# Attention of the second layer in two halves of heads, key masking on GpSimd, and five smaller moves

## The chip, the cores and the metric

The kernel runs on one core of a Trainium2 chip. The metric is the device time of one execution in microseconds, the median of three runs. The core has TensorE (PE in the profile; PEld is its weight load), VectorE (DVE), ScalarE (ACT), GpSimd (POOL) and SyncE (SP), which issues most of the DMAs. Each engine works through its own program in order, and they wait for each other on semaphores.

## The reference

Two transformer layers over 64 blocks (batch entries) of 128 tokens with 256 features, 16 heads of 16 features. Both attend to a context of 128 rows per block. Layer 1 has a mixture of 64 experts behind its attention, layer 2 a gated feed-forward with values rounded to 8 bits.

```python
x = x + tanh(g_xattn[0]) * L0_xattn(layernorm(x), ctx, ctx)            # stage 1
x = x + tanh(g_ffn[0])   * L0_ffn(layernorm(x))                        # stage 2: experts + shared expert
x = x + tanh(g_xattn[1]) * L1_xattn(layernorm(x), ctx, ctx, mask)      # stage 3
x = x + tanh(g_ffn[1])   * L1_ffn(layernorm(x))                        # stages 4 and 5

def L1_xattn(q, k, v, mask):
    query, key, value = heads(q @ wq.T + bq), heads(k @ wk.T + bk), heads(v @ wv.T + bv)
    scores = where(mask == 0, -1e9, query @ key.T / sqrt(16))
    return softmax(scores) @ value @ wo.T + bo

def L1_ffn(x):
    xq = fake_quant(x, clip_x)                                         # needs the maximum of all of x
    h  = fake_quant(silu(xq @ w_gate.T) * (xq @ w_up.T), clip_down)    # needs the maximum of all of h
    return h @ w_down.T
```

## The kernel before

The program has five stages: attention of layer 1, experts, attention of layer 2, pass 0 (gate, up and product of the feed-forward, and its maximum) and pass 1 (rounding, down projection, output). `phase_end` (L269) drains an engine and waits for all five; it stands after the constants (1), after the attention of layer 1 (2), after that of layer 2 (4) and after pass 0 (5).

**Attention.** `attention_pe`, `attention_act`, `attention_dve` and `attention_sp` serve both layers (L is 0 or 1; the profile's stage 3 is L = 1). A block goes through *slots*: in slot s each engine runs its `body` once, each step on the block `stage(lag)` = s - lag. The letters are n (lag -2), g (-1), f (0), m (1), k (2), o (3), w (4), v (5), u (6). The order inside `body` is written out by hand.

A block's scores for all 16 heads take four PSUM banks, `tiles` [128, 4, 512]. Four heads' rows of 32 partitions (two heads of 16, the other masked to zero) lie in four row groups; `scores` (L429) issues for each row group i and half j a matmul of 32 rows and 256 columns into bank i. `maximum` (L933) reduces all four banks to 16 maxima per token with one DVE instruction. `maxima_t` transposes them, `shifted` (L944) adds them to the queries in `qm`. `scores_t` (L446) computes the scores again, transposed, with the maximum taken off, into the same four banks, 16 matmuls of 32 rows and 128 columns. `exponent` (L692) writes their exponential to `pt` with one ACT instruction. In layer 2 `masks` (L421) first writes the mask bias to the banks, before both. `values` (L475) multiplies by the values (16 matmuls into four column groups of 32), `heads_to_tokens` (L561), `head_sums` and `head_norm` (L1038, L1047) and `tokens_to_heads` (L571) normalise, `output` (L544) projects, `residual` (L957) adds. `transposes` (L491) and `project_qk` (L510) make the queries of the coming blocks.

In layer 2 the keys were computed before and come back by DMA (`load_keys_values`, L1216); ACT spreads them into `kp` with four instructions (`mask_keys`, L725), each key copy with the other head's features masked. GpSimd's loop (L2121) does the inverse root of the norm for slot s (`inverse_roots`), adds the experts' outputs of the next block (`experts_sum`, for which DVE's `first_sum` waits) and adds the bias (`add_bias`).

The order of TensorE's body in layer 2 is scores(m), values(o), project_qk(f), transposes(g), scores_t(k), heads_to_tokens(o), output(w), tokens_to_heads(o), maxima_t(m). Scores of m wait for the exponential of k's predecessor, scores_t(k) for the maximum of m: one set of banks serves both.

**The seams.** At the start SP issues the first tile of the context and of x, then eight weight DMAs (`w_in`, L1976), and ends phase 1. GpSimd waits for all of `w_in` (L2083) and clears rows in DRAM with three DMAs (L2104); DVE waits for `w_in` too and runs `scale_queries` (L1993) before the first norm. At the end of layer 2 all engines drain (`phase_end(…, 4)`); then ACT rounds the first chunk of pass 0 (L1794), and in the second chunk's slot calls Silu once on `silu_ready` (L1811), which loads its table. In pass 1 ACT rounds a chunk of 512 tokens in six parts, DVE converts them in three pairs (`whole`, L1907), and TensorE's `down` (L1935) starts when all three pairs are there.

## Time and profile before

| | us |
|---|---|
| median of three runs (lowest, highest) | 1837.52 (1836.88, 1838.45) |
| the profiled execution | 1842.04 |
| its span, first to last instruction | 1840.3 |
| busy in the span: TensorE, DVE, ACT, GpSimd | 1720.2, 1382.6, 1169.1, 668.5 |
| granted TensorE clock, mean | 0.983 |

Attention of layer 1 takes the time up to about 620 us, the experts up to about 1125, attention of layer 2 up to about 1630, pass 0 up to 1756 and pass 1 the rest. The rows further down come from one profiled execution. Times are microseconds from the start of its span; in rows grouped by line the last figure of the mean is nanoseconds. "L527" is line 527. Matmuls overlap, so a busy TensorE is not a full one: the distance from the start of one group to the start of the next says more. A float32 matmul is recorded as two instructions.

### The profile page before, as it was taken

What the parts mean: (1) busy time and instruction counts of PE and PEld (TensorE: products, weight loads), DVE (VectorE), ACT (ScalarE), POOL (GpSimd) and SP (SyncE); (2) the same over time, 40 slices, a digit from 0 to 9 for tenths busy, and PEclk for the clock granted to TensorE, in tenths of its full rate; (3) what the DMA queues carried; (4) which work ended last, traced back from release to release, by engine and by line L of the source; (5) the groups of instructions that cost most, each with busy time, mean ns of one, the idle gap of its engine ahead of it and who ended that gap; (6) DMA issues with size and microseconds to landing.
All of it is one profiled execution on the core that took longest, in us unless ns stands there. A gap on an engine that the chain in (4) does not pass through costs nothing.

```text
span 1840.3 us, 54611 instructions
## 1 busy us (share of the span) xinstructions
PE 1720.2 (93%) x20134; PEld 1343.9 (73%) x20144; DVE 1382.6 (75%) x4582; ACT 1169.1 (64%) x2411; POOL 668.5 (36%) x750
## 2 busy tenths in 40 slices
PE   5999999999999799999999998999999999968845
PEld 4888888888887688888888886677777777733334
DVE  4899999999998546655555544788888888759988
ACT  3777777777777233333323334788888888858875
POOL 1111111111111147777777774222222222211157
PEclk9999999999999899999999998999999999989989
DMA  3233333333334569888988885233332333203274
GB/s 104 83 95 95 95 98 107 98 96 101 98 95 153 173 187 233 220 223 206 223 216 217 216 178 154 83 96 93 89 88 88 89 94 95 69 35 138 103 279 178
DMA packets 231350, 247.64 MB, mean 135 GB/s; under 512 B 29680, under 2 KB 207216, under 8 KB 228912
## 3 DMA queue, kind: packets, MB, share of 16 engines
q1 hardware_dynamic: 206272, 205.54, 34.8%
q0 software_dynamic: 24816, 38.62, 11.6%
q8 instruction: 163, 2.67, 0.6%
q14 instruction: 99, 0.81, 0.1%
HBM read 142.40 MB, written 101.66 MB: 133 GB/s over the span
## 4 chain that ended last, share of the span: by engine, by line
PE 72%; DVE 17%; ACT 8%; issue 1%; SPq 1%; POOL 0%; DMA 0%; POOLq 0%; DVEq 0%; ACTq 0%
DVE mt L940 8%; PE tiles L459 8%; PE tiles L442 8%; PE bank L527 7%; ACT pt L699 6%; PE bank L403 6%; PE tiles L1464 6%; PE bank L383 6%; PE bank L487 4%; PE bank L557 3%; PE tiles L426 3%; PE bank L1478 3%; PE bank L540 3%; PE bank L413 3%; DVE hmax L1852 3%; PE tiles L1446 2%
## 5 line engine op out<-in xcount | busy, mean ns | idle before, releaser
L2091 POOL TENSOR_TENSOR rstd<-var,minus_half 128x2 f32<-128x2 f32 x140 | 97.9, 700 | 650.8 <-DVE var L1020 634.8
L940 DVE TENSOR_REDUCE mt<-tiles 128x16 f32<-128x2048 f32 x128 | 293.5, 2293 | 54.2 <-PE tiles L442 54.1
L699 ACT ACTIVATE pt<-tiles 128x2048 f32<-128x2048 f32 x128 | 240.7, 1880 | 48.1 <-PE tiles L459 48.1
L1639 POOL DMA_INDIRECT accumulator<-ye,tid x128 | 208.5, 1629 | 84.6 <-DVE ye L1583 54.3
L1583 DVE TENSOR_SCALAR ye<-bank,xr 128x256 f32<-128x256 f32 x128 | 56.1, 480 | 154.6 <-PE bank L1478 154.6
L2102 POOL TENSOR_TENSOR res<-res,bias 128x256 f32<-128x256 f32 x128 | 92.9, 725 | 205.8 <-ACT xn L758 203.1
L1624 POOL DMA_INDIRECT xr<-token_rows,tid x128 | 136.9, 1070 | 72.6 <-issue 35.1
L527 PE MATMUL bank<-xt,w_q 128*128 128x128 f32 x1024 | 155.2, 285 | 1.4 <-ACT xt L707 1.4
L459 PE MATMUL tiles<-qm,qkp 32*128 32x128 f32 x4096 | 151.1, 284 | 2.6 <-DVE mt L940 2.6
L442 PE MATMUL tiles<-qkp 32*128 32x256 f32 x2048 | 151.2, 409 | 1.8 <-ACT qkp L721 1.6
L459 PEld LDWEIGHTS tiles<-qm,qkp 32*128 32x128 f32 x4096 | 126.7, 187 | 28.4 <-issue 24.5
L527 PEld LDWEIGHTS bank<-xt,w_q 128*128 128x128 f32 x1024 | 131.9, 195 | 15.6 <-issue 13.6
L487 PE MATMUL bank<-pt,vx 128*32 128x128 f32 x4096 | 140.1, 278 | 1.6 <-ACT at L790 1.0
L487 PEld LDWEIGHTS bank<-pt,vx 128*32 128x32 f32 x4096 | 105.2, 110 | 44.5 <-issue 41.1
L557 PE MATMUL bank<-w_o,at 128*128 128x256 f32 x512 | 133.1, 383 | 1.7 <-ACT at L790 1.7
L952 DVE SCALAR_TENSOR_TENSOR qm<-bank,keep,qkp 128x256 f32<-128x256 f32 x256 | 111.1, 476 | 15.7 <-PE bank L473 15.6
L442 PEld LDWEIGHTS tiles<-qkp 32*128 32x128 f32 x2048 | 87.8, 186 | 40.8 <-issue 27.5
L719 ACT ACTIVATE qkp<-bank,qb 128x128 f32<-128x128 f32 x256 | 88.7, 372 | 36.3 <-PE bank L527 36.2
L675 ACT ACTIVATE res<-bank 128x256 f32<-128x256 f32 x64 | 24.5, 383 | 135.5 <-PE bank L403 135.5
L721 ACT ACTIVATE qkp<-bank,kb,keep 128x128 f32<-128x128 f32 x256 | 106.1, 483 | 0.0
L734 ACT ACTIVATE qkp<-cxax,kb,keep 128x128 f32<-128x128 f32 x256 | 105.4, 485 | 0.0
L557 PEld LDWEIGHTS bank<-w_o,at 128*128 128x128 f32 x512 | 88.0, 192 | 9.5 <-ACT at L790 2.9
(247 smaller groups left out, 4079.9 us busy)
## 6 DMA issues: line engine op xcount, KB each, us to landing
keys_values<-res SPq DMA_DIRECT2D x64, 256.0 KB, 2.9
cxax<-keys_values SPq DMA_DIRECT2D x128, 128.0 KB, 2.5
cxax<-accumulator SPq DMA_DIRECT2D x128, 128.0 KB, 2.2
hidden_away<-h_ring SPq DMA_DIRECT2D x8, 1536.0 KB, 5.0
token_rows<-pay SPq DMA_DIRECT2D x64, 160.0 KB, 1.8
pt<-in_expert_up SPq DMA_DIRECT2D x36, 256.0 KB, 3.5
cxax<-in_ctx SPq DMA_DIRECT2D x64, 128.0 KB, 2.2
res<-in_x SPq DMA_DIRECT2D x64, 128.0 KB, 2.3
```

Of the source, the lines that this page charges most:

```text
L383: last = nc.tensor.matmul(kv_bank(n)[:, k * D:(k + 1) * D], weights_, moving, start=(c == 0), stop=(c == KC - 1))
L403: last = nc.tensor.matmul(shared_bank(n)[:, m * FS + j * P:m * FS + (j + 1) * P], w[:, c, j * P:(j + 1) * P], sxt[n % SHARED_IN][:, c, :], ...
L442: last = nc.tensor.matmul(both, qt[r % 2][rows, j, :], kp[r][rows, :, j, :], start=(L == 0), stop=True, skip_group_check=(L == 1))
L459: last = nc.tensor.matmul(tiles[:, i, n * P:(n + 1) * P], kp[r][rows, e, j, :], qm[rows, e, j, :], start=(L == 0), stop=True, skip_group_c ...
L487: last = nc.tensor.matmul(bank[7][32 * h:32 * h + 32, g * P:(g + 1) * P], vx[r][:, GH * g + h, :], pt[p][:, i, n * P:(n + 1) * P], start=T ...
L527: last = nc.tensor.matmul(o_, w[:, c, j * P:(j + 1) * P], (cx[r] if n else xt[p])[:, c, :], start=(c == 0), stop=(c == KC - 1))
L557: last = nc.tensor.matmul(bank[6][:, 0:D], at[r % 2][:, c, :], w_o[:, c, :], start=(c == 0), stop=(c == KC - 1))
L699: nc.scalar.activation(pt[r % 2][:, :, :], tiles[:, :, :], ACT.Exp).then_inc(sem("exp_done"), 1)
L940: nc.vector.tensor_reduce(mt[:, :].rearrange("p (i n c) -> p i n c", i=RT, n=2 * KC)[:, :, :, 0], tiles[:, :, :].rearrange("p i (n k) -> p ...
L952: last = nc.vector.scalar_tensor_tensor(qm[:, e, :, :], bank[4][:, MAXC[L]:MAXC[L] + P].unsqueeze(1).broadcast_to([P, KC, P]), keep[:, 1 - ...
L1624: nc.gpsimd.indirect_dma_start(out=xr[n % ROWS_IN][:, h, :], out_offset=None, in_=rows[:, :], in_offset=bass.IndirectOffsetOnAxis(ap=tid[n ...
L1639: nc.gpsimd.indirect_dma_start(out=acc[p][:, :], out_offset=bass.IndirectOffsetOnAxis(ap=tid[b % 8][:, h:h + 1], axis=0), in_=ye[r][:, h, ...
```

## The change

**Layer 2.** The 16 heads are treated as two halves h, each in two of the four banks (`tiles[:, 2h:2h+2]`). `half_step(h, m, k, between)` writes both masks, then issues the scores of half h of one block together with the transposed scores of the other half of an older one. Each goes in two pieces u: two row groups serve the scores and the other two the transposed scores, then the roles change; in between stands the work `between`, then a wait of TensorE for the landing of its own first piece. Maximum, exponential and values are cut in two as well. `qm` gets a second buffer in the place of `w_k`. The residual moves one slot back. GpSimd masks the keys. `s_done` and `st_done` now count four per block, `max_done` and `exp_done` two.

```diff
+            def half_step(h, m, k, between):
+                if m is not None:
+                    b, r = m
+                    wait(pe, "exp_done", NB + 2 * (b - 2) + h + 1 if b >= 2 else 0)
+                    mask_half(h, 0)
+                    pe.wait_ge(sem("qk_out_1"), 2 * b + h + 1)
+                    pe.wait_ge(sem("keys_masked"), b + 1)
+                if k is not None:
+                    bt, rt = k
+                    ht_ = 1 - h
+                    pe.wait_ge(sem("max_done"), NB + min(2 * (bt + 1) + ht_ + 1, 2 * NB))
+                    mask_half(ht_, 1)
+                    pe.wait_ge(sem("qm_done"), NB + bt + 1)
+                for u in range(2):
+                    if u == 1:
+                        between()
+                        if m is not None:
+                            pe.wait_ge(sem("s_done"), NB + 4 * b + 2 * h + 1)
+                        if k is not None:
+                            pe.wait_ge(sem("st_done"), NB + 4 * bt + 2 * ht_ + 1)
+                    for e in range(2):
+                        for a_ in range(2):
+                            if m is not None:
+                                i = 2 * a_ + u
+                                rows = slice(32 * i, 32 * i + 32)
+                                n = 2 * u + e
+                                s_last = nc.tensor.matmul(tiles[:, 2 * h + a_, n * P:(n + 1) * P], qt[r % 2][rows, h, :], kp[r][rows, e, h, :],
+                                                          start=False, stop=True, skip_group_check=True)
+                        for a_ in range(2):
+                            if k is not None:
+                                i = 2 * a_ + 1 - u
...
+                    if m is not None:
+                        s_last.then_inc(sem("s_done"), 1)
+                    if k is not None:
+                        t_last.then_inc(sem("st_done"), 1)
...
                 else:
-                    values(o)
+                    half_step(0, m, o, lambda: tokens_to_heads(w))
                     project_qk(f)
                     transposes(g)
-                    scores_t(k)
+                    values_half(0, o)
+                    half_step(1, m, k, lambda: values_half(1, o))
+                    output(w)
                     heads_to_tokens(o)
-                    output(w)
-                    tokens_to_heads(o)
                     maxima_t(m)
...
                 else:
-                    mask_keys(f)
                     normalise_first(g)
                     normalise_second(u)
+                    copy_v(f)
+                    copy_at(w)
+                    exponent_half(1, o)
+                    copy_qk(f)
+                    copy_xt(g)
                     copy_ov(o)
-                    copy_qk(f)
-                    copy_v(f)
-                    copy_xt(g)
-                    exponent(k)
-                    copy_at(o)
+                    exponent_half(0, k)
...
                 else:
-                    maximum(m)
                     first_sum(n)
+                    maximum_half(0, m)
                     first_stats(n)
+                    residual(v)
+                    second_stats(v)
                     variances(n, y)
                     norming(1)
                     token_maximum(u)
+                    maximum_half(1, m)
+                    norming(1)
                     head_sums(o)
                     head_norm(o)
-                    residual(w)
-                    second_stats(w)
                     shifted(m)
-                    norming(1)
...
+            def mask_keys(b):
+                if not 0 <= b < NB:
+                    return
+                r, p = b % 4, b % 2
+                pool.wait_ge(sem(f"kv_in{p}"), 16 * (b - p) + 32)
+                pool.wait_ge(sem("st_done"), NB + 4 * max(b - 3, 0))
+                for j in range(KC):
+                    for e in range(2):
+                        last = G.tensor_scalar(kp[r][:, e, j, :], kvt[p][:, j * P:(j + 1) * P], keep[:, e:e + 1], kb[:, e, j:j + 1],
+                                               ALU.mult, ALU.add)
+                last.then_inc(sem("keys_masked"), 1)
+
             for s in range(NB + PAIR[1]):
                 inverse_roots(pool, 1, s)
+                mask_keys(s - 1)
                 experts_sum(s + 1)
                 add_bias(pool, 1, s)
```

**Norm.** At the start x is loaded before the context; GpSimd no longer waits for the weights, and DVE waits for them and scales the queries only after the first tile's statistics. **Clearing.** The three clearing DMAs of GpSimd move to slot 8 of layer 1. **Drain.** GpSimd no longer drains at the end of layer 2. **Table.** ACT calls Identity once before phase 1 ends and Silu once before phase 4 ends; the call in pass 0 goes. **First chunk.** In pass 1 the first chunk's down projection goes by pairs.

```diff
+                if L == 0 and stage(-2) is not None and stage(-2)[0] == 0:
+                    dve.wait_ge(sem("w_in"), 16 * 8)
+                    scale_queries(dve, 0)
...
-            for dump in (acc[0], acc[1], rows):
-                w = dump.shape[1]
-                G.dma_start(dump[T:T + HALVES * P, :].rearrange("(n p) d -> p n d", p=P), zt[:, :, 0:w]).then_inc(sem("dumps_zero"), 16)
             for s in range(FIRST[0], NB + LAGS):
                 add_bias(pool, 0, s - 2)
                 inverse_roots(pool, 0, s - FIRST[0])
+                if s == 8:
+                    for dump in (acc[0], acc[1], rows):
+                        w = dump.shape[1]
+                        G.dma_start(dump[T:T + HALVES * P, :].rearrange("(n p) d -> p n d", p=P), zt[:, :, 0:w]).then_inc(sem("dumps_zero"), 16)
...
-            phase_end(pool, 4)
+            pool.wait_ge(sem("rstd_step_1"), NORM_STEPS * (NB + PAIR[1] - 1) + 2)
+            pool.sem_inc(sem("phase_done"), 1)
+            pool.wait_ge(sem("phase_done"), PHASES[4])
...
+            act.wait_ge(sem("pool_made"), 3)
+            nc.scalar.activation(silu_ready[:, :], ident[:, 0:1], ACT.Identity)
             phase_end(act, 1)
...
             attention_act(act, 1)
+            act.wait_ge(sem("gates_out"), 1)
+            nc.scalar.activation(silu_ready[:, :], tg[:, 0:1], ACT.Silu)
             phase_end(act, 4)
...
+            def first_down():
+                for p in range(IC // 2):
+                    pe.wait_ge(sem("f_whole"), p + 1)
+                    for t in range(TPC):
+                        for i in (2 * p, 2 * p + 1):
+                            last = nc.tensor.matmul(bank[4 + t][:, 0:D], f_q[0][:, i, t * P:(t + 1) * P], wdi[:, i, :],
+                                                    start=(i == 0), stop=(i == IC - 1))
+                        if p == IC // 2 - 1:
+                            last.then_inc(sem("f_down_done"), 1)
```

## Rows read from the trace of the kernel before

**Rows 1.** Windows of 40 us: window, length, busy of each engine (instructions), clock, DMA, GB/s

```profile
1280.00:1320.00 40.00, 39.26 (x720) 28.73 (x717) 33.33 (x74) 34.49 (x72) 11.34 (x16) 1.00 0.30 88
```

**Rows 2.** Chain of waits by line, 1300 to 1320 us, layer 2

```profile
by line: DVE mt L940 34.6%; ACT pt L699 28.3%; PE tiles L442 16.8%; PE tiles L459 11.5%; PE tiles L426 11.0%; issue 1.7%
```

**Rows 3.** Timeline of TensorE, one slot of layer 2: start, us, engine, line, operation

```profile
1302.19 1.15 PE L442 MATMUL tiles<-qkp 32*128 32x256 f32 x16
1303.27 1.08 PE L487 MATMUL bank<-pt,vx 128*32 128x128 f32 x32
1304.28 1.16 PE L527 MATMUL bank<-xt,w_q 128*128 128x128 f32 x8
1305.27 0.38 PE L507 MATMUL bank<-ident,xn 128*128 128x128 f32 x2
1305.75 0.44 PE L426 MATMUL tiles<-mask_bias,identb 32*32 32x512 bf16 x16
1306.12 1.17 PE L459 MATMUL tiles<-qm,qkp 32*128 32x128 f32 x32
1307.22 0.66 PE L568 MATMUL bank<-ident,ovs 128*128 128x128 f32 x4
1307.72 1.03 PE L557 MATMUL bank<-w_o,at 128*128 128x256 f32 x4
1308.69 0.44 PE L578 MATMUL bank<-ident,on 128*128 128x128 f32 x2
...
1309.29 0.44 PE L426 MATMUL tiles<-mask_bias,identb 32*32 32x512 bf16 x16
1309.66 1.15 PE L442 MATMUL tiles<-qkp 32*128 32x256 f32 x16
```

**Rows 4.** Groups by line, 1200 to 1600 us: busy us, mean ns, idle before

```profile
L940 DVE TENSOR_REDUCE mt<-tiles 128x16 f32<-128x2048 f32 x54 | 123.8, 2293 | 16.0 <-PE tiles L442 16.0
L699 ACT ACTIVATE pt<-tiles 128x2048 f32<-128x2048 f32 x54 | 101.4, 1877 | 37.6 <-PE tiles L459 37.6
L734 ACT ACTIVATE qkp<-cxax,kb,keep 128x128 f32<-128x128 f32 x212 | 87.3, 485 | 0.0
```

**Rows 5.** Timeline of TensorE, three stages of a slot of layer 1

```profile
403.56 0.38 PE L588 MATMUL bank<-ident,pay 128*128 128x128 f32 x2
403.84 0.41 PE L507 MATMUL bank<-ident,xn 128*128 128x128 f32 x2
404.18 1.17 PE L459 MATMUL tiles<-qm,qkp 32*128 32x128 f32 x32
```

**Rows 6.** Groups of GpSimd by line, whole run

```profile
L2102 POOL TENSOR_TENSOR res<-res,bias 128x256 f32<-128x256 f32 x128 | 92.9, 725 | 205.8 <-ACT xn L758 203.1 <-DVE bias L2021 2.6
...
L1824 POOL CAST xq_b<-xq_f 128x1024 bf16<-128x1024 int8 x15 | 15.6, 1040 | 89.7 <-ACT xq_f L1794 89.7
```

**Rows 7.** Chain of waits in order of time, the first 20 us

```profile
5.27 3.55 DMA bias<-in_L_xattn_wo_b
...
11.96 0.75 POOL rstd L2091
13.05 1.28 ACT L758
...
17.00 3.78 PE bank L527 x16
```

**Rows 8.** Timeline at the end of layer 2 and the start of pass 0

```profile
1631.75 0.23 DVE L1667 TENSOR_SCALAR s_gux<-s_gu,scl 128x12 f32<-128x12 f32 x1
1633.29 2.19 ACT L1794 ACTIVATE xq_f<-big,scl 128x1024 int8<-128x1024 f32 x2 [3.85 <-POOLq L271]
...
1636.90 0.99 ACT L1802 COPY xqt<-bank 128x1024 bf16<-128x1024 bf16 x1
```

**Rows 9.** First chunk of pass 1: a row of the timeline, and one of the chain

```profile
1757.55 0.69 DVE L1914 CAST xq_f<-wgi 128x1024 bf16<-128x1024 int8 x1 [1.52 <-ACT wgi L1883]
...
1760.77 5.29 PE bank L1941 x24
```

More of the change, by code:

```diff
@@ L419, in attention_pe, with mask_half @@
             first = L * NB
-            def masks(n):
-                for i in range(RT):
+            def mask_half(h, n):
+                for i in (2 * h, 2 * h + 1):
                     rows = slice(32 * i, 32 * i + 32)
@@ L433, in scores @@
                 b, r = m
-                wait(pe, "exp_done", first + b - 1)
-                if L == 1:
-                    masks(0)
+                wait(pe, "exp_done", b - 1)
                 for j in range(KC):
@@ L441, in scores @@
                         both = tiles[:, i, :].rearrange("p (e c t) -> p e c t", e=2, c=KC)[:, :, j, :]
-                        last = nc.tensor.matmul(both, qt[r % 2][rows, j, :], kp[r][rows, :, j, :],
-                                                start=(L == 0), stop=True, skip_group_check=(L == 1))
+                        last = nc.tensor.matmul(both, qt[r % 2][rows, j, :], kp[r][rows, :, j, :], start=True, stop=True)
                 last.then_inc(sem("s_done"), 1)
@@ L450, in scores_t @@
                 b, r = k
-                pe.wait_ge(sem("max_done"), first + ahead(b, 2))
-                if L == 1:
-                    masks(1)
-                pe.wait_ge(sem("qm_done"), first + b + 1)
+                pe.wait_ge(sem("max_done"), ahead(b, 2))
+                pe.wait_ge(sem("qm_done"), b + 1)
                 for j in range(KC):
@@ L715, in copy_qk @@
                 act.wait_ge(sem("qk_done"), first + b + 1)
-                wait(act, "st_done", first + b - 3)
+                if L == 0:
+                    wait(act, "st_done", b - 3)
                 wait(act, "qm_done", first + b - 1)
@@ L723, in copy_qk @@
                     last.then_inc(sem(sm("qk_out")), 1)
-            def mask_keys(f):
-                if f is None:
-                    return
-                b, r = f
-                p = r % 2
-                act.wait_ge(sem(f"kv_in{p}"), 16 * (b - p) + 32)
-                wait(act, "st_done", first + b - 3)
-                for j in range(KC):
-                    for e in range(2):
-                        nc.scalar.activation(kp[r][:, e, j, :], kvt[p][:, j * P:(j + 1) * P], ACT.Identity, bias=kb[:, e, j:j + 1], scale=keep[:, e:e + 1])
             def copy_v(f):
@@ L1809, in body @@
                         quantise(stage(0))
-                        if stage(1) == 0:
-                            nc.scalar.activation(silu_ready[:, :], sig[:, 0:1], ACT.Silu)
                     if i == 4:
```

67 lines of the change are left out of this document (52 added, 15 removed).

## The prediction

> **What bounds the kernel now.** I read the stretches of the run first, then the chain of waits, then single slots. The program has five stages: attention of layer 1, experts, attention of layer 2, and two passes of the last feed-forward. The change works on the third, and on four seams: the start, the end of layer 2, the first chunk of pass 0 and that of pass 1.
>
> In layer 2 no engine is full: of 40 us TensorE shows 39.26, DVE 33.33, ACT 34.49 [rows 1]. The chain of waits says why [rows 2]: it goes round masks and scores, maximum, masks and transposed scores, exponential, all on the same four PSUM banks. Its round is from one scores start to the next, 1309.66 - 1302.19 = 7.47 us [rows 3]. The pieces fit: masks .37 and scores till they have landed 1.15, maximum 2.29, masks .37 and transposed scores 1.17, exponential 1.88 [rows 3, 4] make 7.23, and the rest are hand-overs. TensorE fills its free time in this chain with values, projection, transposes and output. "39.26 of 40" must not be read as full: ends are modelled. The reader should look at starts.
>
> **How much TensorE work there is in a slot.** From start to start [rows 3]: scores 1.08, values 1.01, projection .99, transposes of the next tile .48, masks .37, transposed scores 1.10, heads to tokens .50, output .97, then .60 for three transposes up to the masks, then .37. In layer 1, where nothing waits, two transposes take .28, and .34 where the next stage has another tiling [rows 5]. So of the .48 some .14 is waiting for the maximum, of the .97 some .05 for the normalised heads, of the .60 some .17 for the exponential: about .36 in all. The work is 7.47 - .36 = 7.11 us.
>
> **The change in layer 2.** With halves the maximum of one half runs beside the exponential of the other, and both beside TensorE. The chain no longer closes: after the second part of the first half step come projection, transposes and half the values (.99 + .34 + .56 = 1.89 us), against half an exponential (.94 and some .1 fixed) and half a maximum (1.15 and .1). After the second half step come output and heads to tokens, 1.38 us, against the same 1.25 and a landing of .1. That is just enough. So the .36 of waiting goes, and what is late next is TensorE's own work.
>
> That work grows. Scores (8 matmuls of 256 columns) and transposed scores (16 of 128) become four pieces of 8 matmuls of 128 columns, with other work between the pieces; values are cut in two. The transposed scores are 16 matmuls in 1.10 [rows 3]. Four matmuls run side by side, one in each row group; each is written as two records of 284 ns. First start to last end is 1.17, so the eighth group of records starts 1.17 - .284 = .89 after the first, about .115 per group with .08 more for the first (it waits for its weights), and the next stage starts .21 after that, .1 more than a group's time. A piece of half the size is then .08 + 4 x .115 + .10 = .64, not .55. Values have no such first step: 1.01 whole, 1.01 - 4 x .115 = .55 half. Piece by piece, in the new order: masks .37, piece .64, tokens to heads .33, piece .64, projection .99, transposes .34, half values .55, masks .37, piece .64, half values .55, piece .64, output .95, heads to tokens .43, one transpose .20: 7.64 us. Before it was 7.11, so .53 is added, for four more changes of tiling: half step | tokens to heads | half step, half step | half values | half step, and the two ends. I take these full, since TensorE works in order and rows 3 and 5 show the steps at every such boundary, whether it had waited or not.
>
> The new wait of TensorE on its own first piece (s_done, st_done) has the inserted work as cover: the piece lands .07 after the inserted one starts, which lasts .33 or .55. It costs nothing; without the inserted work it would cost about .3 twice a slot. Behind it stand all later matmuls.
>
> A rule speaks against this change: the Trainium skill, TensorEngine Tiling (Array Packing), Tiling Modes, says that changing the tiling mode drains the engine. By that rule the four boundaries are paid, as in my 7.64. Another page, the Trainium skill, TensorE: Matmul & The Clock Gate, Part 3, prices concurrent tiles at one matmul's duration and about 4 ns per tile more, and by that alone halves cost half, and the slot would be the 7.11 of the first rival.
>
> ACT loses four key masks (4 x .485 = 1.9) and gains one fixed part: 34.49 / 40 x 7.47 = 6.4 falls to about 4.7. DVE gains one fixed part of about .1: 33.33 / 40 x 7.47 = 6.2 becomes 6.4 [rows 1, 4]. It has slack against 7.64, but little where order matters: maximum, small norm, head sums, head norm, shift, first sum must pass in the 3.5 us from half step to half step. Keys masked, GpSimd: no row shows such an instruction. Bounds are 1024 one-input elements in 1.04, which is .13 for 128, and .73 for a whole two-input instruction of 256 [rows 6]; half of the latter, .36, is nearest, so 4 x .36 = 1.5 us per slot. Behind the four stands the sum of the experts' outputs (.73), for which DVE's first sum waits, and behind that one the maximum. Between the variance and the first sum of the next slot DVE's order has token maximum, half maximum, small norm, head sums, head norm and shift, over half of a slot of 7.64, about 4.0 us with its wait; .70 (inverse root) + 1.5 + .73 = 2.9 fits. It fits up to .64 per instruction; above that each .1 costs .4 a slot. SP's loads now wait for masks made two slots earlier: nothing.
>
> Slots: 64, of which three run while the pipeline fills and the clock is lower. 61 x (7.64 - 7.47) = +10.4. Filling brings longer TensorE slots at 1.2 GHz, and GpSimd's four instructions ahead of norm steps: -1 to +3, I take +1; draining has half exponentials but the same number of slots: 0.
>
> **The seams.** *Start.* The first inverse root came at 11.96, behind the weights, which land at 5.27 + 3.55, and behind three clearing DMAs of GpSimd, since GpSimd and DVE waited for the weights [rows 7]. Now the norm needs only x, whose load is issued first. The phase ends at about 5.9, after SP's last issue at 5.27, so the first inverse root is at about 7 and the first tile is normalised at 8.6; the 1.28 of table load is past by then. Then the value projection is last (weights 8.9, slow clock, to 11.0), its copy, transposes, copy of xt: projection at about 12.6 and not 17.00. -4.4, bounds -3 and -5. Clearing at slot 8 goes into GpSimd, which is idle most of a layer-1 slot: 0; with no such idle time 2.5.
>
> *Drain and table.* Pass 0 starts rounding at 1633.29, released by GpSimd's drain, though DVE's scales are ready at 1631.98 [rows 8]. Without it DVE's own drain is next, about 1632.1: -1.2. The Silu table no longer delays the copy at 1636.90, which could start at about 1636.4: -.5. Loaded earlier it lies under DVE's last steps.
>
> *First chunk of pass 1.* TensorE began at 1760.77, after the third pair, and ran 5.29 us to 1766.06 at the slow level, while the first pair was ready at 1758.24 [rows 9]. By pairs it does a third (1.76) at 1758.3, and ends about 1763.6. DVE's next steps take back a little: -2.0, bounds 0 (if ACT's rounding is what holds chunk two) and -2.4. Seams together -8.1, bounds -5 and -9.
>
> **Sum.** +10.4 + 1 - 8.1 = +3.3. Against the profiled execution, 1842.0 becomes 1845.3; its span is 1840.3, and the median of the runs is 4.5 lower than the profiled one, so the median goes from 1837.5 to about 1841.
>
> **The rivals.**
> *Half pieces cost half (0.30).* If drains and first weight loads overlap with neighbouring stages, TensorE's work stays near 7.11, at most 7.35. For it: between transposes and transposed scores in layer 1 only .06 is seen [rows 5]. Against it: the .21 between a row-tiled piece's last start and the next stage, in both layers. Time: 61 x (-.36 to -.12) + 1 - 8.1 gives 1808 to 1823, centre 1816.
> *The engines catch on each other (0.17).* The other side: DVE's stretch of 3.5 us has almost no slack, and the single transpose waits for the second half maximum. If each slot loses a further .2 at the hand-over DVE to TensorE before that transpose, the slot is 7.85, and +23 + 1 - 8.1 gives 1853. It decides from the point where half a maximum takes over 1.3 us, or the first sum ends later than the first half's scores.
> *GpSimd is late (0.06).* At .8 per mask instruction, .6 a slot are lost: over 1875.
> *It doesn't do what it says (0.02).* If the halves still ran one after another, two fixed parts more, 7.8: 1850.
> My forecast, TensorE-bound at 7.64, has 0.45. Its own range is 7.53 to 7.76: 1834 to 1849.
>
> **How the numbers follow.** 0.2% is 3.7 us, about what a measurement of this kernel can tell from no change: 1833.8 to 1841.2. The forecast's case gives same 0.20, slower 0.22, faster 0.03. The first rival gives faster 0.30, the second slower 0.15 and same 0.02, the others slower 0.08. Together faster 0.33, same 0.22, slower 0.45. The range is 1814 to 1857: it leaves out the lower part of the first rival and most of the late GpSimd.
>
> **What would show it.** Right: a layer-2 slot of 7.6 to 7.7; TensorE's stages start to start without idle time before the masks; each half piece .62 to .66; DVE waiting for scores before each half maximum; first projection near 12.6; pass 0 rounding about 1.2 us after DVE's last scale minus .1. Wrong: half pieces of .55 and a slot near 7.1 (first rival), idle time of TensorE before the single transpose or the masks released by DVE (second), DVE's first sum waiting for GpSimd (third). Most at risk is the .09 that each half piece is over half of a whole: 1 us in the sum is .016 per slot.

## The result, and the profile after

| | before | after | ratio, 95% interval |
|---|---|---|---|
| median of the runs (4 each) | 1837.99 us | 1864.38 us | 1.0145 [1.0126, 1.0163] |
| range of the runs | 1836.88 to 1838.91 | 1862.45 to 1872.07 | |
| profiled execution | 1842.04 | 1862.74 | |
| its span | 1840.3 | 1861.0 | |

The changed kernel is slower by 1.45%: 26.4 us between the medians, 20.7 between the two profiled executions. What follows explains the 20.7, which can be laid out stretch by stretch. The other 5.7 is the spread of single executions around their medians, and no trace shows it.

**A slot of layer 2.** First the window of 40 us, as in [rows 1], and the shares of the chain of waits, as in [rows 2]. Columns of the window: length, then busy us of TensorE, its weight loads, DVE, ACT and GpSimd with their instructions, the granted clock, the share of DMA, GB/s.

```profile
1280.00:1320.00 40.00, 40.00 (x781) 29.59 (x777) 32.16 (x78) 27.01 (x53) 19.25 (x35) 1.00 0.31 90
```

```profile
by line: PE tiles L457 31.7%; PE bank L581 16.3%; PE bank L540 14.4%; PE tiles L427 10.9%; PE bank L611 10.6%; PE bank L632 5.5%; PE bank L622 4.4%; PE bank L561 3.3%; PE tiles L464 2.7%; PE bank L511 1.5%
```

DVE and ACT, which held 34.6% and 28.3% of the chain before [rows 2], are gone from it. It is TensorE alone, from stage to stage. The next rows are one slot on TensorE, as [rows 3] were before: start, us, engine, line. L427 are the masks, L457 and L464 a piece of scores and of transposed scores side by side, L632 tokens to heads, L581 projection, L561 transposes, L540 half the values, L611 output, L622 heads to tokens, L511 the transpose of the maxima.

```profile
1299.93 0.43 PE L427 MATMUL tiles<-mask_bias,identb 32*32 32x512 bf16 x16
1300.29 0.38 PE L457 MATMUL tiles<-qkp 32*128 32x128 f32 x2
...
1300.50 0.28 PE L457 MATMUL tiles<-qkp 32*128 32x128 f32 x2
...
1300.62 0.28 PE L457 MATMUL tiles<-qkp 32*128 32x128 f32 x2
...
1300.95 0.44 PE L632 MATMUL bank<-ident,on 128*128 128x128 f32 x2
1301.31 0.38 PE L457 MATMUL tiles<-qkp 32*128 32x128 f32 x2
...
1301.97 1.16 PE L581 MATMUL bank<-xt,w_q 128*128 128x128 f32 x8
1302.97 0.38 PE L561 MATMUL bank<-ident,xn 128*128 128x128 f32 x2
1303.28 0.65 PE L540 MATMUL bank<-pt,vx 128*32 128x128 f32 x16
1303.85 0.43 PE L427 MATMUL tiles<-mask_bias,identb 32*32 32x512 bf16 x16
1304.22 0.38 PE L457 MATMUL tiles<-qkp 32*128 32x128 f32 x2
...
1304.87 0.65 PE L540 MATMUL bank<-pt,vx 128*32 128x128 f32 x16
1305.45 0.38 PE L457 MATMUL tiles<-qkp 32*128 32x128 f32 x2
...
1306.10 1.13 PE L611 MATMUL bank<-w_o,at 128*128 128x256 f32 x4
1307.07 0.60 PE L622 MATMUL bank<-ident,ovs 128*128 128x128 f32 x4
1307.51 0.31 PE L511 MATMUL bank<-ident,mt 128*128 128x128 f32 x1
1307.75 0.43 PE L427 MATMUL tiles<-mask_bias,identb 32*32 32x512 bf16 x16
```

From masks to masks 1307.75 - 1299.93 = 7.82 us, against 7.47 before, and no row has idle time before it. Read a piece from inside: from its first group of four matmuls to the second .21 (1300.29 to 1300.50), then .12 and .11, and .22 from the last group's start to the next stage (1300.73 to 1300.95).

**Stretch by stretch**, from the same points of both traces:

| stretch | before | after | difference |
|---|---|---|---|
| start of the span to the last whole maximum of layer 1 (DVE) | 591.39 | 587.13 | -4.3 |
| from there to the first norm of layer 2 (ACT, xn) | 539.84 | 537.91 | -1.9 |
| first norm to the second block's (first half) exponential | 26.76 | 32.58 | +5.8 |
| sixty slots behind that | 448.06 | 469.21 | +21.1 |
| from there to the rounding of pass 0 | 27.24 | 29.22 | +2.0 |
| rounding of pass 0 to that of pass 1 | 122.83 | 121.68 | -1.2 |
| pass 1 to the end | 84.18 | 83.27 | -0.9 |

They sum to +20.6, the difference of the spans but for rounding. The -1.9 is no work of the change: 600 to 610 us was granted .66 of the clock before, and 1.00 after (first before, then after).

```profile
600.00:610.00 10.00, 8.36 (x84) 5.83 (x82) 5.01 (x33) 4.36 (x8) 2.82 (x6) 0.66 0.23 77
600.00:610.00 10.00, 8.52 (x72) 6.45 (x71) 7.49 (x53) 4.02 (x10) 2.47 (x5) 1.00 0.47 139
```

Of the thirteen other profiled runs with the new start, nine took 519.2 to 519.8 us from the last maximum of layer 1 to the last expert output and four 521.4 to 521.8, as did both with the old start (521.6 and 521.4). It comes and goes between executions and is worth 2 us; that the old start favours it can't be excluded on two runs. Of the -1.2 between the two roundings .5 is the table (below). The rest goes with the granted clock in the first 10 us of pass 0, .60 after and .51 before; max first, which was granted .50 there, took 122.64.

**The seams.** The start, as in [rows 7], in the chain of waits:

```profile
5.23 3.77 DMA bias<-in_L_xattn_wo_b
9.02 0.43 DVE w_q L2074
...
12.85 3.26 PE bank L581 x16
```

The projection starts at 12.85 in place of 17.00, and what releases it is again the arrival of the weights, by way of DVE's scaling and the second tile's norm. The first inverse root starts at 6.94, the first tile is normalised at 8.63, and the value projection ends at 11.2, all near the forecast. The end of layer 2, as in [rows 8]:

```profile
1653.33 1.28 ACT L2241 ACT_TABLE_LOAD   x1
1655.62 0.23 DVE L1735 TENSOR_SCALAR s_gux<-s_gu,scl 128x12 f32<-128x12 f32 x1
1656.05 2.19 ACT L1862 ACTIVATE xq_f<-big,scl 128x1024 int8<-128x1024 f32 x2 [1.22 <-DVEq L272]
...
1659.18 1.01 ACT L1870 COPY xqt<-bank 128x1024 bf16<-128x1024 bf16 x1 [0.95 <-PE bank L1837]
```

Rounding starts .20 behind DVE's last scale, where it was 1.31, so 1.1 is gained. The copy comes 3.13 behind the rounding and not 3.61, so the table's .5 is gained too.

### The profile page after: what moved, and what is told of

It reads as the page before. It is cut to its first block, busy times and chain, and to the rows that moved or that the text cites. A ratio compares the mean times of both kernels' runs of the same rounds, so it can differ in the third digit from the quotient of the medians.

```text
span 1861.0 us, 57243 instructions
## 1 busy us (share of the span) xinstructions
PE 1756.5 (94%) x21168; PEld 1377.9 (74%) x21168; DVE 1387.5 (75%) x4646; ACT 1100.4 (59%) x2220; POOL 778.9 (42%) x1006
## 4 chain that ended last, share of the span: by engine, by line
PE 85%; DVE 10%; ACT 1%; issue 1%; DMA 1%; POOL 1%; SPq 1%; POOLq 0%; DVEq 0%; ACTq 0%
PE bank L581 10%; PE tiles L457 8%; PE bank L611 6%; PE bank L404 6%; PE tiles L1532 6%; PE bank L384 6%; PE bank L540 4%; PE tiles L496 4%; PE tiles L482 4%; PE bank L525 3%; PE bank L1546 3%; PE bank L594 3%; PE bank L414 3%; PE bank L622 3%; DVE hmax L1918 3%; PE tiles L427 3%
## 5 line engine op out<-in xcount | busy, mean ns | idle before, releaser
L1004 DVE TENSOR_REDUCE mt<-tiles 128x8 f32<-128x1024 f32 x128 | 156.9, 1226 | 85.1 <-PE tiles L457 85.1
L457 PE MATMUL tiles<-qkp 32*128 32x128 f32 x2048 | 186.7, 300 | 0.6 <-PE tiles L464 0.4
L457 PEld LDWEIGHTS tiles<-qkp 32*128 32x128 f32 x2048 | 137.2, 189 | 54.7 <-issue 51.9
L993 DVE TENSOR_REDUCE mt<-tiles 128x16 f32<-128x2048 f32 x64 | 146.8, 2293 | 29.9 <-PE tiles L482 29.7
L581 PE MATMUL bank<-xt,w_q 128*128 128x128 f32 x1024 | 156.0, 286 | 0.9 <-ACT xt L770 0.9
L762 ACT ACTIVATE pt<-tiles 128x1024 f32<-128x1024 f32 x128 | 131.2, 1025 | 31.7 <-PE tiles L464 25.7
L611 PE MATMUL bank<-w_o,at 128*128 128x256 f32 x512 | 138.5, 393 | 1.7 <-ACT at L843 1.7
L581 PEld LDWEIGHTS bank<-xt,w_q 128*128 128x128 f32 x1024 | 132.6, 196 | 9.5 <-ACT xt L770 1.6
L834 ACT COPY ovs<-bank 128x512 f32<-128x512 f32 x128 | 77.8, 608 | 100.4 <-PE bank L540 98.0
L753 ACT ACTIVATE pt<-tiles 128x2048 f32<-128x2048 f32 x64 | 120.6, 1884 | 1.2 <-PE tiles L496 1.2
L2209 POOL TENSOR_SCALAR qkp<-cxax,keep,kb 128x128 f32<-128x128 f32 x256 | 111.1, 448 | 0.0
L843 ACT COPY at<-bank 128x256 f32<-128x256 f32 x128 | 47.7, 372 | 90.8 <-PE bank L632 90.6
L611 PEld LDWEIGHTS bank<-w_o,at 128*128 128x128 f32 x512 | 87.1, 190 | 17.0 <-ACT at L843 2.7
L811 ACT ACTIVATE xn<-res,nmr,rstd 128x256 f32<-128x256 f32 x128 | 76.9, 601 | 31.7 <-DVE nmr L1090 25.9
```

Of the source, the lines that this page charges most:

```text
L457: s_last = nc.tensor.matmul(tiles[:, 2 * h + a_, n * P:(n + 1) * P], qt[r % 2][rows, h, :], kp[r][rows, e, h, :], start=False, stop=True, ...
L581: last = nc.tensor.matmul(o_, w[:, c, j * P:(j + 1) * P], (cx[r] if n else xt[p])[:, c, :], start=(c == 0), stop=(c == KC - 1))
L611: last = nc.tensor.matmul(bank[6][:, 0:D], at[r % 2][:, c, :], w_o[:, c, :], start=(c == 0), stop=(c == KC - 1))
L753: nc.scalar.activation(pt[r % 2][:, :, :], tiles[:, :, :], ACT.Exp).then_inc(sem("exp_done"), 1)
L762: nc.scalar.activation(pt[r % 2][:, 2 * h:2 * h + 2, :], tiles[:, 2 * h:2 * h + 2, :], ACT.Exp).then_inc(sem("exp_done"), 1)
L993: nc.vector.tensor_reduce(mt[:, :].rearrange("p (i n c) -> p i n c", i=RT, n=2 * KC)[:, :, :, 0], tiles[:, :, :].rearrange("p i (n k) -> p ...
```

## The experiments

A short name for each follows. *Full-width* is the order of the kernel before in layer 2. "Fill" is the time from the first norm of layer 2 to the second block's exponential, or its first half: 26.76 us before, 32.58 after. Ratios are against runs of the kernel before on the same chip in the same session.

**The two parts of the change.** The first run takes the seams alone, the second the halves and GpSimd's key masks alone; each is the kernel before with that part of the diff.

> Only the seams of the change: start (GpSimd no longer waits for the weights, clearing moved), drain of GpSimd, SiLU table, first chunk of pass 1. Layer 2 is that of the kernel before. Theory (the parts add, and the stages of the changed kernel's trace price them: start and layer 1's end -6.2, seam behind layer 2 -1.1, table -0.5, first chunk -0.9): 8.7 us under the kernel before, 1829.3 us, ratio 0.9953, with the slot of layer 2 at 7.47 us. Rival 1 (layer 1's end gains only the start's 4.2, since 1.5 of the 6.2 is a stretch at full clock that comes by chance): 1831. Rival 2 (layer 2 or its wait for the experts swallows an earlier start): 1835 or more.

> Only the second layer of the change (halves of heads, keys masked by GpSimd), with the seams of the kernel before. Theory (parts add): 1864.4 + 8.7 = 1873 us, ratio 1.019, slot of layer 2 7.82 us. If the seams' gains depend on the halves: another number, between 1864 and 1868.

Measured: seams alone 1835.41 us, 0.9969 [0.9958, 0.9981]; layer 2 alone 1870.70 us, 1.0161 [1.0144, 1.0178]. So -.31% and +1.61% against +1.45% for both: the parts add within their intervals, and all of the loss is layer 2's. The seams came out at -5.3 us and not -8.7. In this profiled run (also 5.3 under that of the kernel before) the low stretch at 600 us was there again (521.55 us), as rival 1 had it, 1.6 more went in the first blocks of layer 1 (its exponentials at 30.14 and 59.57, against 34.81 and 62.61 before), and pass 1 gained .2 in place of .9 (below). The slot was 7.47 and 7.82 us.

**Key masks by GpSimd without halves, and halves without GpSimd.**

```
 scores(m), layer 2 of full_pool_masks:
+    pe.wait_ge(sem("keys_masked"), b + 1)
 attention_act, layer 2:
-    mask_keys(f)
 GpSimd's loop:
     inverse_roots(pool, 1, s)
+    mask_keys(s - 1)
     experts_sum(s + 1)
```

> The seams, and full-width layer 2 with its keys masked by GpSimd in place of ScalarE, in the place that the change gives them in GpSimd's program. Theory P (the 7 to 8 us beyond the slots that layer 2 cost in the changed kernel are a fill in which the inverse roots and expert sums of the next blocks queue behind four key masks of 0.45 us a block): the slot stays at 7.47 us, since DVE's maximum and ACT's exponential bind it, and the kernel is 4 to 8 us over the run with the seams alone, about 1835. Theory H (the fill's cost is that of the halves on TensorE): as the run with the seams alone, within 1 us, 1829. Also possible: a shorter slot, as ScalarE gives off about 1.1 us a slot; then 7.3 to 7.4 us a slot and 4 to 8 us less.

> The changed kernel with the key masks given back to ScalarE, at the head of its slot as in the kernel before; halves and seams stay. Theory P (GpSimd's queue makes the fill): slot 7.82 us as in the changed kernel (ScalarE has 5.3 of 7.8 us busy and takes about 1.1 more), fill 6 to 8 us shorter, 1857 us. Theory H (halves make the fill): 1864 us as the changed kernel. If ScalarE then comes late with an exponential: slot over 7.9 us and 1870 or more.

Measured: full-width with GpSimd's masks 1832.01 us, 0.9952 [0.9935, 0.9968]; halves with ACT's masks 1863.61 us, 1.0129 [1.0112, 1.0146]. Theory P falls twice. The first is 3.4 us under the seams alone, more than the 1 us that theory H allowed: 1.15 is the fill, and in this profiled run the stretch at 600 us had the full clock, worth 2. With GpSimd's masks the full-width fill is 25.59 us, shorter by 1.15 than with ACT's (26.74 in the run with the seams), and with ACT's masks the fill of the halves is 32.89, no shorter than 32.58. The full-width slot in this run: the window, the shares of the chain in 1300 to 1320 us, and two exponentials of the timeline.

```profile
1280.00:1320.00 40.00, 39.26 (x734) 28.69 (x719) 33.33 (x75) 26.77 (x48) 20.56 (x37) 1.00 0.30 90
```

```profile
by line: DVE mt L930 34.5%; ACT pt L701 28.3%; PE tiles L444 16.8%; PE tiles L461 12.3%; PE tiles L426 11.0%; issue 1.8%
```

```profile
1300.12 1.88 ACT L701 ACTIVATE pt<-tiles 128x2048 f32<-128x2048 f32 x1 [0.69 <-PE tiles L461]
1307.58 1.88 ACT L701 ACTIVATE pt<-tiles 128x2048 f32<-128x2048 f32 x1 [0.69 <-PE tiles L461]
```

ACT's busy time falls from 34.49 of 40 [rows 1] to 26.77, and the slot stays at 7.46: the same chain with the same shares as [rows 2]. 1.4 us of ACT's work a slot was worth nothing, since ACT was only in the chain with its exponential.

**Where TensorE's slot grows.** Three runs keep all matmuls and move stages.

```
 swap_values:
     project_qk(f)
+    values_half(0, o)
     transposes(g)
-    values_half(0, o)
 merge_values:
     transposes(g)
-    values_half(0, o)
-    half_step(1, m, k, lambda: values_half(1, o))
+    wait for exp_done of the first half
+    half_step(1, m, k, lambda: (values_half(0, o), values_half(1, o)))
 no_between:
-    half_step(0, m, o, lambda: tokens_to_heads(w))
+    tokens_to_heads(w)
+    half_step(0, m, o, nothing)
     ...
-    half_step(1, m, k, lambda: values_half(1, o))
+    half_step(1, m, k, nothing)
+    values_half(1, o)
```

> The changed kernel with the first half of the values moved next to the second half, between the two pieces of the second half step: the same matmuls, one stage border less a slot (8 in place of 9 places where TensorE goes from one shape of tile to another or from one stage to the next). Theory B (the 0.18 us a slot that the forecast missed, and most of what halves cost, lies at the borders of stages, 0.1 to 0.15 us each): slot 7.82 down to 7.67 to 7.72 us, 6 to 9 us in all. Rival C (the matmuls themselves cost more, borders nothing): slot within 0.03 of 7.82.

> The changed kernel with the first half of the values ahead of the transposes of the normed rows, so between project and transposes, which have one shape of tile: the same matmuls, one change of shape more a slot. Theory B: slot 7.92 to 7.97 us. Rival C: 7.82.

> The changed kernel with nothing between the two pieces of a half step: transposes of the tokens ahead of the first half step, second half of the values behind the second. Two changes of shape fewer (the four stage borders of the two insertions become two), but the wait of a piece for the one before it, which the insertion hides, is bare twice a slot. Theory B: minus 0.25, plus twice 0.1 to 0.3 for the bare wait: 7.75 to 8.15 us a slot; if the bare wait costs less than a change of shape, under 7.82. Rival C: 8.0 to 8.4, the bare waits alone.

*Swap*: 1873.50 us in one run; sixty slots in (1637.70 - 1158.13) us, 7.99 a slot, +.17 for one border more. TensorE's timeline shows where:

```profile
1305.66 1.16 PE L581 MATMUL bank<-xt,w_q 128*128 128x128 f32 x8
1306.74 0.64 PE L540 MATMUL bank<-pt,vx 128*32 128x128 f32 x16
1307.32 0.44 PE L561 MATMUL bank<-ident,xn 128*128 128x128 f32 x2
1307.69 0.43 PE L427 MATMUL tiles<-mask_bias,identb 32*32 32x512 bf16 x16
```

From projection to values 1.08 and not 1.00, transposes .37 and not .31. Theory B holds, at a little more than it asked, and C falls. The Trainium skill, TensorEngine Tiling (Array Packing), Tiling Modes, says that changing the tiling mode drains the engine, which the forecast had weighed. The runs agree in that such a border costs time, .17 us here; they don't show what the engine does in it.

*Merge*: 1867.05 us, 1.0156 [1.0138, 1.0173], slot 7.83 to 7.86 where B wanted 7.67 to 7.72. The two halves of the values together take 1.01 and not .57 + .58, so the border is saved, .14. But .03 comes back on the transposes, which now stand before the masks (.34 for .31), and .11 on the masks, here the row of their weight loads:

```profile
1304.28 0.28 PEld L427 LDWEIGHTS tiles<-mask_bias,identb 32*32 32x32 bf16 x16 [0.17 <-ACT pt L763]
```

The masks write the banks that ACT's half exponential reads, and this ran until 1304.16. The half values that stood there were the cover of that exponential. So the halves have a second bound right beside TensorE's work: at a slot of 7.8 there is no room to save a border in this place.

*No between*: 1944.98 us in one run, slot 9.11, outside what both theories allowed. The two rows of TensorE that wait:

```profile
1302.30 0.38 PE L457 MATMUL tiles<-qkp 32*128 32x128 f32 x2 [0.21 <-PE tiles L464]
1305.91 0.44 PE L632 MATMUL bank<-ident,on 128*128 128x128 f32 x2 [0.70 <-DVE on L1119]
```

Two pieces with their bare wait take 1.58 us, against .65 + .65, so the wait costs .27 twice (the forecast had said about .3). The rest, .75, I had not thought of: tokens to heads now comes right behind heads to tokens and waits for DVE's normalised heads, which the first half step used to cover: from the transpose of the maxima to tokens to heads it is .98 and not .24. 7.82 + .54 + .75 = 9.11, and no other stage changed by more than .01, so fewer borders gave nothing back: a piece pays its slow first group after a wait for its own engine as it does after another tiling.

**The fill.**

```
 warm_halves, behind transposes(g) of the first four blocks:
+    for _ in range(3):
+        nc.tensor.matmul(bank[7][:, :], identb, mask_bias[:, 0, :, :], start=True, stop=True)
 max_first, DVE in layer 2:
+    maximum_half(0, m)
     first_sum(n)
-    maximum_half(0, m)
```

> The changed kernel, and behind the transposes of the first four blocks of layer 2 three matmuls of 128x512 bf16 whose result nobody reads (12 in all, about 2.6 us of TensorE at full clock). Theory F (the fill is dear since TensorE is granted 0.50 of its clock from 1130 to 1145 and from 1150 to 1155, each stage then taking twice its time, and more of the halves' fill than of the full-width one is TensorE's): if the added work keeps the clock at full, the first half exponential comes 14 to 18 us behind the first norm in place of 21.95, and the kernel is 3 to 6 us faster than the changed one, about 1859 where that takes 1864. If the clock falls all the same, 2.6 to 5 us slower. Rival D (the fill is one of waits and depth, not of the clock): first half exponential no earlier.

> The changed kernel with VectorE's maximum of the first half ahead of its sum of x and the experts' rows (as in the full-width order), so that the maximum doesn't stand behind a sum that waits for GpSimd. Theory Q (queue: in the first slots the first half's maximum starts at 1135.60, behind a sum that waits for GpSimd's key masks and expert sum, though its scores were done by 1131.7): first half exponential 18 to 19 us behind the first norm in place of 21.95. Theory E (TensorE's own chain of half pieces at 1.2 GHz ends at about the same time, as it does with the masks on ScalarE, 22.3): 21.3 to 22.3. Slot 7.82 in both.

> As the run before, and with the matmuls of the earlier run behind the transposes of the first four blocks, which held the clock at full until 1134. If the fill is two chains side by side, GpSimd's with VectorE's order and TensorE's at 1.2 GHz, this takes from both: first half exponential 20.0 to 21.5 us behind the first norm, where each alone leaves 21.3 or more. If the fill has one cause, the added matmuls change nothing beside the run before, or cost up to 1 us.

*Warm*: 1862.49 us, 1.0129 [1.0110, 1.0148]. The clock fell later, not never: .96 in 1130 to 1135, where the changed kernel had .50, then .50 and .51 up to 1145, as there. The first half exponential came no earlier, 22.85 us behind the first norm against 21.95; TensorE's idle time before the first transpose of maxima grew from 1.69 to 2.30 us instead. Rival D, for this stretch; the 2.6 to 5 us that the added work was to cost didn't come either.

*Max first*: 1861.88 us in one run, fill 30.65 us, 1.9 less. Two rows of DVE in the changed kernel, and then the same two with the other order:

```profile
1134.74 0.93 DVE L1045 TENSOR_TENSOR res<-res,cxax 128x256 f32<-128x256 f32 x1 [2.26 <-POOL cxax L2198]
1135.60 1.21 DVE L1004 TENSOR_REDUCE mt<-tiles 128x8 f32<-128x1024 f32 x1
```

```profile
1132.29 1.23 DVE L1004 TENSOR_REDUCE mt<-tiles 128x8 f32<-128x1024 f32 x1
1134.62 0.93 DVE L1045 TENSOR_TENSOR res<-res,cxax 128x256 f32<-128x256 f32 x1 [1.11 <-POOL cxax L2198]
```

The maximum no longer stands behind a sum that waits for GpSimd, and starts 3.3 us earlier. The first exponential gained only .5 of it (21.46), as theory E had it. The other 1.4 came on the way to the second block's, 9.19 us against 10.63, and there .77 of the clock was granted in 1150 to 1155, where the changed kernel had .50. Five other runs of the halves took 10.5 to 10.6 for it, in either order. So the order is worth some .5. *Warm and max first*: 1865.53 us, first exponential 21.93, fill 32.51. The two don't add; the clock fell again at 1141 for the stages behind. The forecast for it, 20.0 to 21.5, was wrong.

> Halves, key masks on ScalarE, and VectorE's maximum of the first half ahead of its sum. No key mask stands in GpSimd's queue. Theory T (what is left of the fill's excess is TensorE's: the scores of one block are four pieces of 8 matmuls in which only two of the four row groups work while nothing transposed runs beside them, 2 x 2.52 us at 1.2 GHz against 2.02 for the full-width scores): second block's first half exponential 30 to 32 us behind the first norm of layer 2. Theory G (GpSimd's queue makes the rest): 27 to 28.

> Halves, key masks on GpSimd but behind the expert sum and the output bias of their step, and VectorE's maximum of the first half ahead of its sum. Theory T: 30 to 31 us from the first norm to the second block's first half exponential, as with the order of VectorE alone (30.65). Theory G: 27 to 29. If the masks, now last, hold back the scores themselves: over 31.5.

*With ACT's masks and max first* (one run, 1867.46 us) the fill is 31.96: no key mask is in GpSimd's queue, and 5.2 of the 5.8 us are still there. DVE's maxima wait for TensorE in it. *With GpSimd's masks last* (one run, 1866.10 us) it is 35.75, since the first scores then wait 1.38 us for their masked keys. So GpSimd's masks don't make the fill's excess, and theory G falls; 31.96 is within theory T's 30 to 32. What TensorE does in the fill, first before, then after, each at 1.2 GHz (granted .50):

```profile
1136.10 2.02 PE tiles L442 x16
```

```profile
1134.62 2.52 PE L457 MATMUL tiles<-qkp 32*128 32x128 f32 x16
```

Before, one block's scores are 2.02 us. After, the row is one half of a block, and the block has two, with projection (2.08) and transposes (.63) between them. In the steady slot the other two row groups work on transposed scores beside them; in the fill there are none, and the half step is hardly shorter (at 2.4 GHz 1.42 us from its first piece to the next stage, in max first, against 1.58 with transposed scores beside it and the same bare wait, in no between). The full-width maximum (2.29) ran beside projection and transposes. The halves' second one runs behind everything.

But TensorE's speed alone doesn't set the first exponential. In layer 2 alone the clock was full up to 1140, and both half steps of the first block took 1.49 and 1.50 in place of 2.52. The exponential came 22.15 us behind the first norm, no sooner than the 21.95 of the changed kernel. TensorE waited instead:

```profile
1140.22 1.50 PE L457 MATMUL tiles<-qkp 32*128 32x128 f32 x16
1145.17 0.48 PE L511 MATMUL bank<-ident,mt 128*128 128x128 f32 x1 [3.45 <-DVE mt L1004]
```

DVE's second half maximum stands behind the first one and a norm there, and these behind the sum that waits for GpSimd (till 1141.09). So two chains of about the same length lead to the first exponential, TensorE's and this one, and shortening either leaves the other; warm and max first, which took from both, still needed 21.93. What they share is that the second half's scores and maximum come behind the projection and the next block's transposes. That this order makes up the 5.8 us is argued from the rows; what the runs show is that GpSimd's masks don't, and that neither a faster TensorE nor DVE's order alone takes more than .5 off the first exponential.

**The first chunk of pass 1, and GpSimd's order in the full-width version.**

> The version with the seams and full-width layer 2 whose keys GpSimd masks, and the first chunk of pass 1 put back as in the kernel before. Theory K (the early start of the first chunk is lost again in the second, whose 24 matmuls take 4.1 to 5.3 us in place of 2.79 at a lower granted clock): no difference, ratio 0.9952 as with the new chunk, plus or minus 0.0005. The forecast's step (first chunk worth 2.0 us): 1.5 to 2 us slower, ratio 0.9962.

> The same version, and GpSimd's key masks behind the expert sum and the output bias of their step in place of ahead of them. If the masks delay the norms of the next blocks in a way that the end feels: first exponential 15 to 16 us behind the first norm in place of 16.69, 1 us faster. If the chain of the first slots is TensorE's at half clock: 16.7 and no difference.

Measured: 1833.12 us, 0.9966 [0.9952, 0.9980] with the old chunk; 1834.34 us, 0.9962 [0.9949, 0.9974] with masks last (first exponential 17.19 us behind the first norm, not 16.69). Neither can be told from 0.9952, and the first lies even nearer to the 0.9962 of the forecast's step than to theory K's 0.9952. The traces settle the chunk better. TensorE's first three chunks, with the new order (after) and then with the old one (layer 2 alone, the third cut by the window); the first rounding of pass 1 is at 1777.73 and 1786.80:

```profile
1780.01 4.46 PE L2016 MATMUL bank<-wdi,xq_f 128*128 128x256 bf16 x24 [4.04 <-DVE xq_f L1980]
1787.57 4.12 PE L2007 MATMUL bank<-wdi,f_sgp 128*128 128x256 bf16 x24 [3.10 <-DVE f_sgp L1980]
1793.24 2.79 PE L2007 MATMUL bank<-wdi,xq_f 128*128 128x256 bf16 x24 [1.56 <-DVE xq_f L1980]
```

```profile
1791.45 5.28 PE L2006 MATMUL bank<-wdi,xq_f 128*128 128x256 bf16 x24 [6.42 <-DVE xq_f L1979]
1797.85 2.79 PE L2006 MATMUL bank<-wdi,f_sgp 128*128 128x256 bf16 x24 [1.12 <-DVE f_sgp L1979]
1802.49 0.72 PE L2006 MATMUL bank<-wdi,xq_f 128*128 128x256 bf16 x5 [1.84 <-DVE xq_f L1979]
```

With the new order the second chunk starts 9.84 us behind the first rounding and not 11.05, so 1.2 is won. But it then takes 4.12 us in place of 2.79, as TensorE's 24 matmuls start at the lower level, after an idle time of 3.10. The third chunk starts at 15.51 against 15.69, so .2 is left. Over all profiled runs it started at 15.46 to 15.71 with the new order (eleven runs, and two at 16.13 and 16.14), and at 15.44, 15.68 and 15.69 with the old one: nothing is gained. Theory K. In the kept version pass 1 took 83.47 with the new order and 83.20 with the old.

**The version to keep** is the full-width one with the seams and GpSimd's key masks, 0.9952 [0.9935, 0.9968] of the kernel before: 8.7 us faster than that, and some 35 faster than the changed one. Whether GpSimd's masks beat ACT's there is open, as the intervals overlap; the trace gives them 1.15 us in the fill.

## Why the prediction was wrong

It said 1841 us, with 1814 to 1857; it is 1864. Slower was the likeliest side, the size was not. Term by term, in the profiled execution (forecast +3.3, measured +20.7):

- *The chain opens and TensorE's work bounds the slot*: right. No stage of TensorE waits in the slot, and DVE's half maxima wait for scores.
- *Slot 7.64*: mis-sized, 7.82. The piece was nearly right (.64, measured .65 to .66). The miss is spread over the order: tokens to heads .36 for .33, half values .57 and .58 for .55, the single transpose .24 for .20, output, projection and heads to tokens .01 to .02 each, transposes .03 under. I had taken the moved stages at their price among stages of their own shape, and priced only four new borders. The swap says what one border is worth, .17; how the rest divides over the others no run shows. In a slot with one engine in series each hundredth is .6 us in the sum: +21.1 and not +10.4. This is the largest part of the error, 10.7 us. (The upper end of the forecast's own range, 7.76, makes 1848 by its sum, not 1849.)
- *Filling +1, bounds -1 to +3*: wrong, +5.8. I had thought of longer slots and of GpSimd's queue. The step that failed is the half step's price where it has no partner: with scores alone it is hardly shorter, so at 1.2 GHz a block's scores take 2 x 2.52 and not 2.02, and the second half, with its maximum, comes behind projection and transposes. Without GpSimd's masks 5.2 us stay. How the 5.8 divides between TensorE's chain and DVE's behind GpSimd stays open.
- *Draining 0*: wrong, +3.1 (the +2.0 of the table and the seam's 1.1 in it). The same number of slots, but a block is now finished a good half slot later: the last block's exponentials start at 1640.59 and 1644.08, 3.49 apart, where one of 1.88 us stood.
- *Start -4.4*: right, -4.2 at the projection, nearly for the reason given (the copy of xt waited .3 more behind the second tile's norm). *Drain -1.2 and table -.5*: right, -1.1 and -.5. *Clearing 0*: nothing seen of it.
- *First chunk -2.0, bounds 0 and -2.4*: at the bound, 0. Of the .9 that pass 1 was shorter in the profiled execution, .7 lies in one later chunk of the kernel before that took 4.10 us instead of 2.79, with .73 and .56 granted. The new order gives its gain back in chunk two by the granted clock, and not by ACT's rounding as the bound had supposed.
- *GpSimd's instruction .36, threshold .64*: .448, fits in the steady slot. What the third rival named, DVE's first sum waiting for GpSimd, does occur, but only in the fill.
- *Half pieces cost half (0.30)*: fell. In a piece the first and the last group cost .21 and .22 and only the two between .12, four times a slot.
- *The engines catch (0.17)*: its time, 1853, is nearer than mine, by another road. Nothing waits at the hand-over it named, though the second half maximum ends (1307.44) only .07 before the transpose that needs it. The catch is real, too, one step on: merging the values ran into ACT's half exponential at once.
- *The median*: I had put it 4.5 under the profiled execution, as before. After it lies 1.6 over it.

## What to carry to other kernels

When a chain over shared banks is opened by cutting stages in half, count every border that one in-order engine gets, also those of stages that are only moved, and price each from a row with the same neighbours on both sides. Then run the pipeline's first and last block by hand: work that was paired in the steady slot is alone there and costs nearly the same, and what was put behind another stage comes later by that stage. Taking work off an engine that is in the chain with one instruction only gives nothing in the slot, and an earlier start of TensorE on a small piece can be lost again in the next piece, at the lower clock.

## What the runs showed of the hardware

- One more change of tile shape on TensorE cost .17 us in a full fp32 slot (7.82 to 7.99).
- Two pieces of scores alone, one right behind the other, took 1.42 us from their first start to the next stage's at 2.4 GHz (max first), and 1.58 with as many transposed scores beside them (no between): twice the matmuls for a ninth more time.
- GpSimd's mask of 128x128 fp32 with a scale and a bias from columns took .448 us, and ACT's .485 [rows 4].
- Twelve added matmuls of 512 bf16 columns in the fill, three behind each of four blocks' transposes: granted clock 1.00 and .96 in 1125 to 1135, where the changed kernel had .81 and .50, then .50 in both. The first exponential came no earlier.
- The same stretch of layer 1, 600 to 610 us, was granted .66 in one execution and 1.00 in another, which moved all that follows by 2 us.
